# Cross-attention and a mixture of experts on one core: TensorE's groups ordered by type, and an input loaded earlier

## The reference

```
scores = Q @ K.T / sqrt(8) + bias(|i - j|)
x = x + softmax(scores) @ V @ Wo.T + bo
probs = softmax(xf @ Wr); topk_p, topk_i = top_k(probs, 2)
y_e = silu(xf @ Wg[e]) * (xf @ Wu[e]) @ Wd[e]
x = x + shared(xf) + sum_e c[e] * y_e
```

## Time and profile before

| | |
|---|---|
| median of 3 runs | 237.85 us (237.54 to 238.19) |
| profiled execution: its own time | 236.51 us |
| its span on the core | 234.7 us |
| TensorE clock granted | 1.000 of full speed, in the whole span |
| busy: TensorE, its weight loads, VectorE | 91%, 75%, 75% |
| busy: ScalarE, GpSimd | 51%, 32% |
| DMA | 20.24 MB, 86 GB/s on average |
| first score product of the steps (start, us) | 37.23, 61.02, 86.06, 111.36, 136.03, 161.14, 185.79 |

### The profile page before, as it was taken

One profiled execution on the slowest core, in us unless ns is written; L12 is line 12 of the kernel. 1 busy time (PEld: TensorE's weight loads), 2 busy tenths in 40 slices (PEclk: granted clock), 3 DMA queues, 4 the chain that ended last, 5 costly groups with the idle time before them and its releaser, 6 DMA issues.

```text
span 234.7 us, 6077 instructions
## 1 busy us (share of the span) xinstructions
PE 214.3 (91%) x1938; PEld 175.2 (75%) x1938; DVE 175.5 (75%) x612; ACT 118.9 (51%) x283; POOL 74.3 (32%) x178
## 2 busy tenths in 40 slices
PE   2979866979999999999999999999999899989995
PEld 2757444757888777977897888878887679768884
DVE  4589526995799678985899569967885788654891
ACT  8566645376336734474346543663367334763310
POOL 2520007010770159012931095107800580037000
DMA  5653488245113350327042701452134500350000
GB/s 158 173 89 105 102 155 270 73 93 140 43 35 81 117 128 0 106 52 201 0 102 49 188 13 56 92 135 68 34 87 104 135 0 4 78 131 0 1 25 22
DMA packets 13079, 20.24 MB, mean 86 GB/s; under 512 B 2800, under 2 KB 9440, under 8 KB 12544
## 3 DMA queue, kind: packets, MB, share of 16 engines
q1 hardware_dynamic: 12624, 18.77, 31.9%
q10 hardware_dynamic: 432, 1.19, 1.7%
HBM read 16.03 MB, written 3.78 MB: 84 GB/s over the span
## 4 chain that ended last, share of the span: by engine, by line
PE 41%; issue 33%; DVE 10%; POOL 9%; ACT 3%; DMA 1%; DVEq 0%; POOLq 0%; SPq 0%; ACTq 0%
PE ps_up L525 8%; PE ps_m L553 8%; PE ps_pv L458 4%; PE ps_st L439 4%; PE ps_up L530 4%; DVE nmax L977 4%; POOL hid L1324 3%; PE ps_pv L465 3%; DVE tg L1081 2%; DMA ident<-in_c_ident 1%; PE ps_s L381 1%; PE ps_m L480 1%; POOL xb L1306 1%; PE ps_st L486 1%; PE ps_st L493 1%
## 5 line engine op out<-in xcount | busy, mean ns | idle before, releaser
L801 ACT ACTIVATE th<-ps_up 128x256 f32<-128x256 f32 x72 | 27.6, 384 | 39.1 <-PE ps_up L530 38.6
L553 PE MATMUL ps_m<-wd_sb,hid 128*128 128x128 f32 x288 | 44.8, 283 | 0.2 <-DVE hid L1223 0.2
L977 DVE TENSOR_REDUCE nmax<-ps_s 128x4 f32<-128x512 f32 x64 | 42.1, 682 | 1.4 <-PE ps_s L381 0.8
L749 ACT ACTIVATE probs<-ps_st 128x512 f32<-128x512 f32 x64 | 36.8, 592 | 11.2 <-PE ps_st L439 10.9
L1081 DVE SCALAR_TENSOR_TENSOR tg<-th,ps_up 128x256 f32<-128x256 f32 x72 | 29.8, 414 | 13.2 <-ACT th L801 12.9
L553 PEld LDWEIGHTS ps_m<-wd_sb,hid 128*128 128x128 f32 x288 | 37.5, 191 | 1.4 <-DVE hid L1223 0.4
L1324 POOL TENSOR_TENSOR hid<-hid,crep 128x256 f32<-128x256 f32 x54 | 37.7, 730 | 0.2 <-issue 0.2
L1087 DVE TENSOR_TENSOR hid<-tg,ps_up 128x256 f32<-128x256 f32 x72 | 29.8, 413 | 1.0
L525 PE MATMUL ps_up<-x_hi,wg_hi 128*128 128x256 f32 x72 | 26.6, 369 | 0.4 <-ACT x_hi L782 0.2
L439 PE MATMUL ps_st<-stacks_sb 98*128 98x128 f16 x256 | 24.9, 220 | 0.4 <-DMA stacks_sb<-nmT 0.3
L1288 POOL TENSOR_TENSOR ve<-mv,eps_sb 128x1 f32<-128x1 f32 x16 | 3.1, 191 | 69.2 <-DVE mv L1028 69.2
(11 more groups left out here) (148 smaller groups left out, 433.7 us busy)
## 6 DMA issues: line engine op xcount, KB each, us to landing
crep<-cw_dram SPq DMA_DIRECT2D x28, 256.0 KB, 4.5
stacks_sb<-qk_dram SPq DMA_DIRECT2D x32, 128.0 KB, 3.3
qk_dram<-qk_parts SPq DMA_DIRECT2D x16, 128.0 KB, 1.8
out_y<-x_all SPq DMA_DIRECT2D x8, 128.0 KB, 4.2
wg_sb<-in_wgT ACTq DMA_DIRECT2D x1, 576.0 KB, 4.1
wu_sb<-in_wuT ACTq DMA_DIRECT2D x1, 576.0 KB, 3.4
wd_sb<-in_wd SPq DMA_DIRECT2D x1, 576.0 KB, 4.0
x_all<-in_x SPq DMA_DIRECT2D x2, 256.0 KB, 4.2
```

Source lines behind the costliest of these rows:

```text
L553: last = mm(ps_dn[:, b * P:(b + 1) * P], hid[:, buf, c, b * P:(b + 1) * P], wd_sb[:, c, :], start=(c == 0 and b == 0), stop=(c == SHARED), ...
L749: fn(probs[:, b, g * HG * P:(g + 1) * HG * P], scores_bank(a, g)[:], ACT.Exp).then_inc(exp_sb, 1)
L801: fn(th[:, c % 2, :], ps_up[c % 2][:, 0, :], ACT.Tanh, scale=0.5).then_inc(tanh_sb, 1)
L977: v.tensor_reduce(nmax[:, b, HG * g:HG * g + HG], ps_s[g % 2][:].rearrange("p (h j) -> p h j", h=HG), AX_X, ALU.max, negate=True).then_inc ...
```

## The change

Three things. TensorE's list in the first half of a step is reordered, so that two score groups, two up chunks or two down chunks stand side by side. VectorE's x2_low(f) and row_max(a, 0, 2) change places. SyncE issues the load of x of groups 2 and 3 behind the stacks of group 0, once these have landed, and no longer in load_more. The instructions are the same ones in number and kind.

```diff
             def load_more():
                 sp.wait_ge(s_nm[0], 16)
                 sp.wait_ge(s_nm[1], 16)
-                sp.dma_start(x_all[:, 2 * NB:4 * NB, :], x[:, 2 * NB:4 * NB, :]).then_inc(s_x, 16)
                 sp.dma_start(ctx_all[:, 2 * T:4 * T], ctxT[:, 2 * T:4 * T]).then_inc(s_ctx, 16)
...
             stack_k(0, 0)
             stack_q(0, 0)
+            sp.wait_ge(s_stack, 64)
+            sp.dma_start(x_all[:, 2 * NB:4 * NB, :], x[:, 2 * NB:4 * NB, :]).then_inc(s_x, 16)
             step(None, 0, 1, 2, 0)
...
                 late_down(0)
+                late_down(1)
                 scores(a, 0, 2, abuf)
-                late_down(1)
+                scores(a, 0, 3, abuf)
                 expert_in_T(f)
-                scores(a, 0, 3, abuf)
                 late_down(2)
                 up(f, 0)
+                up(f, 1)
                 scores(a, 1, 0, abuf)
-                up(f, 1)
                 scores(a, 1, 1, abuf)
                 shift_T(a, 0)
                 router(f)
+                up(f, 2)
                 late_down(3)
+                late_down(4)
                 scores(a, 1, 2, abuf)
-                up(f, 2)
-                late_down(4)
                 scores(a, 1, 3, abuf)
                 up(f, 3)
                 late_down(5)
                 scores_T(a, 0, 0, abuf)
+                scores_T(a, 0, 1, abuf, f=f)
                 late_down(6)
-                scores_T(a, 0, 1, abuf, f=f)
+                late_down(7)
                 shift_T(a, 1)
-                late_down(7)
                 second_half(f, a, p, q, abuf)
...
                     hidden(f - 1, 8, abuf)
+                row_max(a, 0, 2)
                 x2_low(f)
-                row_max(a, 0, 2)
                 row_max(a, 0, 3)
```

## The result

The changed kernel takes 233.14 us (median of 4 runs, 232.61 to 234.20); beside it the kernel before took 237.69 (4 runs, 237.33 to 238.19). The ratio is 0.9841, 95% interval 0.9807 to 0.9874: 4.55 us less. The forecast was 234.5, so 3.35 less than the median it started from.

What follows compares the result with a forecast made beforehand. VectorE's unbroken row of work up to cw was taken to set a step's first half. Start 0.7, first step 0.3 and six steps 2.3 sum to 3.3, from 237.85 to 234.5; own range 233.6 to 235.6, wider range 233.0 to 236.9.

Steps and rivals of the forecast that it cites:

- x loaded earlier: In the start, VectorE's 3.71 us wait for x goes; 0.7 of a possible 1.47 gained, as the wd copy limits.
- Row maxima around x_lo: In each step, a row maximum fills VectorE's idle time ahead of x_lo; mean gain 0.38, six steps give 2.3.
- The rule of the Trainium skill on shared access: In a step, max_low waits for GpSimd's weighing, so the gain is 0.43; without it six steps give 1.6 more.
- Pairs on TensorE: In a step, three fewer entries into 32-bit work save 0.18; second up block saves 0 to 0.09, taken as 0.
- The 0.4 that the prediction would take off the sum: If type changes cost nothing, pairs save nothing: sum smaller by 0.4, from two end steps where TensorE comes last.
- Rival (b): More than forecast: wd load up to 0.8 earlier, second up blocks save 0.6 over seven steps; 233.1, chance 0.13.
- Rival (a): Only the start helps; GpSimd's boundaries or row_max(a, 1, 2) waiting for scores keep steps' length; 236.85, chance 0.2.
- a sign that the forecast is wrong: x_lo later behind x_hi, second-block maxima waiting for TensorE, or steps keeping their length; no size given.
- Rival (c): Slower: row_max(a, 1, 2) starves as x_lo comes 0.64 late; seven steps cost 1.8; 238.95, chance 0.04.
- First step: In the step from 37.23, the maximum fills idle time but gate(f, 0) waits for tanh; 0.3, between 0 and 0.64.
- The sum: Whole kernel: 0.7 + 0.3 + 2.3 = 3.3; the profiled execution would go from 236.5 to 233.2.
- The median of the runs is 237.85, 1.3 above it; I subtract there: Whole kernel: the 3.3 is taken from the runs' median, not the profiled 236.5, giving 234.5.

Runs made afterwards that it cites:

- e1: The kernel before with the earlier load of x alone: 235.99 us, beside 237.10 for before.
- e7: e6 with ScalarE's copy of wd moved behind tanh(0,1) of the first step, and fewer fillers ahead of x2n's transposes: 232.46 us.
- e5: The kernel before with 21 filler transposes in three idle times of TensorE in the start: 236.51 us.
- e3: The kernel before with VectorE's swap of x2_low and row_max(a, 0, 2) alone: 235.47 us, beside 237.10 for before.
- e9: e6 with GpSimd weighing one column of each expert chunk in place of 256: 231.75 us.
- e10: e5 with GpSimd weighing one column of each expert chunk in place of 256: 234.23 us.
- e11: e6 with scores(a, 1, 0) between up(f, 0) and up(f, 1) again: 233.39 us.
- e6: The changed kernel with 18 filler transposes in the same three idle times of TensorE in the start as e5: 233.33 us.
- e0: The changed kernel run once more, nothing altered, beside later experiments: 235.80 us, beside 237.21 for before.
- e2: The changed kernel with the load of x back in load_more, both new orders kept: 235.98 us, beside 237.10 for before.
- e4: The kernel before with TensorE's new order alone, VectorE's list and the load as before: 238.03 us, beside 237.10 for before.

## Why the prediction was right, and where its size was off

- **x loaded earlier, 0.7.** Right, to 0.3. Taken alone it gave 0.9 (its profile) to 1.15 (its runs at full clock, e1). The wd copy set the limit at 37.92 where 37.7 was forecast (the load took 4.3 to land in place of 4.0), x2n came at 38.99, forecast 38.8. Moving the copy away gave the rest, 0.87 (e7). That the load is free was right: wu landed later beside it, and ScalarE's idle time still covered that (1.42 left before nmT, at 24.61, where it was 2.12).
- **Row maxima around x_lo, 2.3.** Right in mechanism and place, and near in size. In the worked step gate came at 91.83 (forecast 91.86), max_low from 92.17 to the end of the weighings, shift_T at 92.66 (92.68), cw 0.44 earlier (0.43). Over six steps 149.89 stands against 152.35: 2.46; against the executions of the old order in e1 and e5 it is 1.9 to 2.0. Most of the gap between these two figures is the first of the six: in that execution of before max_high met a weighing there (0.80 long) and in e1 and e5 it did not (0.17). Against e5 the first of the six is even 0.27 longer in the changed kernel, where both instructions wait, and the other five are 0.3 to 0.6 shorter: a loss of this kind is what the mean of 0.38 allowed for, and against e5 the mean is 0.33. The swap alone gives the gain (e3).
- **The rule of the Trainium skill on shared access** ("SBUF — State Buffer", Who interferes with whom), that a VectorE instruction with two SBUF inputs waits until the GpSimd instruction that reads SBUF has ended, and that a cast can take the shared pair too: the trace agrees for both. max_low and the cast max_high fall to 0.17 as soon as GpSimd reads one column (e9, e10), from up to 0.44 and 0.71. That the six steps would give 1.6 more without max_low's wait was too much: with neither of the two waiting they are 1.2 shorter (148.72 against 149.89), and the change as a whole is worth less, not more, since TensorE's scores come next.
- **Pairs on TensorE, 0.18 in a step.** They are there on TensorE (0.13 against 0.22 for the first product of a second block, so the upper bound of 0.09 was the true one), and are worth 0.1 in all. The 0.09 can't be put down to a change of type, since a first product takes 0.20 behind the router's fp32r products too; what makes it is open. The Trainium skill ("TensorE: Matmul & The Clock Gate", Step-by-step: what each phase is for) names no cost for a change of type; the only row against that is the 0.06 of the earlier trace rows, and for the time it made no difference. The 0.4 that the prediction would take off the sum by it is in none of the sum's terms. Rival (b) was wrong in both halves: its 0.09 exists but isn't on the path (e11), and the wd load did not come forward.
- **Rival (a)**, that row_max(a, 1, 2) waits for its scores, is true of the third, fifth and sixth of the six steps, at 0.2, 0.2 and 0.98. I had worked out "nothing to spare" from one step, and it was so. The prediction also named such a wait as a sign that the forecast is wrong. It came, and these three steps shrank all the same: 24.36, 24.02 and 27.09 against 24.67, 24.65 and 27.58. Rival (c) is this mechanism too; it did not reach its price.
- **First step, 0.3.** e6 against e1: 24.03 against 24.36, so 0.33. This is from one execution of each, and e6 has the new order of TensorE and the fillers as well; no run has the swap alone in this step at full clock.
- **The sum, 3.3**, is 3.18 at full clock (e5 against e6). The terms as measured, some 1.1, 0.3 and 2.0, add to 3.4. The profiled execution of before, at 1.000, took 236.51, and the three runs of the changed kernel at 1.000 took 232.61, 233.14 and 233.14.
- **The step that was mis-sized** is "The median of the runs is 237.85, 1.3 above it; I subtract there". I treated the 1.3 as a constant offset. It was mostly the clock: 53 of 63 later runs of before had a mean clock under 0.998 and took 0.9 or 1.5 longer than the others, and the one profiled execution was at 1.000. Three of the four runs of the changed kernel kept their clock, and so its median lost 1.2 more than the sum.
- **What was luck.** Three of four at full clock was a good draw. Beside the later runs one of six kept it, in spite of the shorter idle time ahead of attn's transpose (0.68 for 2.14), and over all ten executions the changed kernel's median is 234.2, against 237.1 for the 63 of before: 2.9 less. The clock did hold more often with the early load: 10 of 22 runs with it and without fillers kept 0.998 or more (changed, e0, e1), and 14 of 99 without it (before, e2, e3, e4). The measured 233.14 lies below the forecast's own range of 233.6 to 235.6 and on the 233.1 of rival (b), though neither of (b)'s two reasons is behind it.

## What to carry to other kernels

When a profile and the median of the runs differ by half a per cent, find out by what before you carry the difference along as a constant; the granted clock of each run tells. An edit that fills or opens an idle time of TensorE of 1 to 2 us has two prices, its own and that of the clock, and a few filler products in a free bank part the two. Two instructions changed places gave nearly all that the steps gained: look for work that has its operands and stands behind a wait, on the engine that the others wait for, and for the engine that is 0.06 behind it before you count on more. A reordering that frees an engine which nobody waits for can still move the one group that another engine will want next.

## What was not expected of the hardware

- TensorE's clock fell to 0.50 in some executions of one program and not in others. In the profiles it stayed there for 3 to 4 us (6 to 7 in e2), behind idle times of 0.5 to 2.1 us, and TensorE was busy all through most of that time. For the kernel before, runs at a mean granted clock of 0.991 to 0.993 took 0.9 us more than those at 0.998 or more, and runs at 0.985 took 1.5 more; for the changed kernel the difference was 1.1 to 1.4 at 0.992 and 4.0 at 0.977.
- One DMA issue can take long, and what stands behind it is late. In the profile of e6_fill_after the second of the six steps is longer by 1.06 than in the changed kernel: SyncE took 1.57 to issue one DMA that takes 0.46 or 0.47 in the other steps of that execution and at most 0.90 in the other profiles, so nmT's rows were late for the transposed scores (timelines of SyncE and TensorE, e6_fill_after). This is why its six steps sum to 150.75.

```profile
91.90 1.57 SPq L223 DMA_DIRECT2D qk_dram<-qk_parts  x1
```

```profile
96.17 0.40 PE L440 MATMUL ps_st<-stacks_sb 98*128 98x128 f16 x4 [1.07 <-DMA stacks_sb<-nmT]
```
